# A new order of all engines for a patch-embedding, retention, attention and expert-routing kernel

## The reference

```python
tokens = concat([cls, patches(x) @ W + b]) * pos_embed        # 64 patches of 28x28x3 = 2352 values
h = concat([tokens, txt], axis=1)                             # 97 tokens a sample
a = layernorm(h)
q, k, v = a_heads @ wq, a_heads @ wk, a_heads @ wv            # complex, 8 heads of 16
y = (((q k^T) * decay_mask) v).real                           # causal
yn = groupnorm(y) * gn_scale + gn_bias
h = h + ((silu((a @ w1).real) * yn) @ w2).real
z = layernorm(h); o = softmax(qz kz^T / 4) vz @ Wo + bo       # 8 heads of 16
t = layernorm(z + o) * ln1_g + ln1_b
e = argmax(t @ gate_W + gate_b); gw = max(softmax(...))       # one of 8 experts for each token
h = h + gw * (gelu(t @ W1[e] + b1[e]) @ W2[e] + b2[e])
```

## Time and profile before

| | us |
|---|---|
| three runs | 1279.16, 1279.10, 1278.93 (median 1279.1) |
| profiled execution, own time | 1276.99 |
| its span (first to last instruction) | 1275.0 |
| PE busy | 1240.5 (97%) |
| DVE busy | 998.1 (78%) |
| ACT busy | 794.3 (62%) |
| POOL busy | 410.5 (32%) |
| mean granted TensorE clock | 0.991 |

### The profile page before, as it was taken

How to read it: one execution, slowest core, us unless ns; L and a number is a source line. 1 busy time by engine, 2 the same in 40 slices (tenths; PEclk the granted TensorE clock), 3 DMA queues, 4 the chain that set the end, 5 groups by cost and what they waited for, 6 DMA issues and landing times.

```text
span 1275.0 us, 43269 instructions
## 1 busy us (share of the span) xinstructions
PE 1240.5 (97%) x15924; PEld 930.4 (73%) x15925; DVE 998.1 (78%) x2447; ACT 794.3 (62%) x1787; POOL 410.5 (32%) x268
## 2 busy tenths in 40 slices
PE   8999999999999999999999999999999876999998
PEld 6667777777777777777777777777776556999998
DVE  3678888888888888888888888888888766777776
ACT  2466666666666666666666666666666664556555
POOL 0000322232222222222222222222222146666666
PEclk9999999999999999999999999999999898999999
DMA  9522333333333333333333333333330013443332
GB/s 387 188 83 80 93 93 93 93 93 93 93 93 93 93 93 93 93 93 93 94 92 93 93 93 94 93 93 94 93 93 16 14 17 89 135 114 102 103 103 62
DMA packets 95146, 124.80 MB, mean 98 GB/s; under 512 B 56619, under 2 KB 77149, under 8 KB 94592
## 3 DMA queue, kind: packets, MB, share of 16 engines
q1 hardware_dynamic: 38400, 102.47, 25.4%
q0 software_dynamic: 56576, 19.93, 7.5%
HBM read 101.27 MB, written 20.82 MB: 96 GB/s over the span
## 4 chain that ended last, share of the span: by engine, by line
PE 80%; DVE 6%; issue 5%; DVEq 3%; POOL 2%; DMA 2%; ACT 1%; SPq 0%; POOLq 0%; ACTq 0%
PE bank_emb L479 22%; PE bank_s L550 10%; PE bank_x L564 7%; PE bank_y L460 7%; PE bank_s L637 4%; PE bank_s L614 4%; PE bank_z L460 4%; PE bank_y L649 3%; PE bank_y L667 3%; DVEq L1842 2%; PE bank_z L597 2%; DVE home_x L1846 2%; PE bank_s L460 2%; PE bank_y L690 1%; PE bank_s L843 1%
## 5 line engine op out<-in xcount | busy, mean ns | idle before, releaser
L1909 POOL DMA_INDIRECT expert_rows<-row_sb,placei x128 | 278.1, 2173 | 562.8 <-issue 464.8
L479 PE MATMUL bank_emb<-home_x 128*128 128x256 f32 x1216 | 338.1, 392 | 0.0
L479 PEld LDWEIGHTS bank_emb<-home_x 128*128 128x128 f32 x1216 | 210.3, 189 | 81.9 <-issue 56.5
L1374 DVE TENSOR_TENSOR home_s<-bank_s,con 97x776 f32<-97x776 f32 x256 | 239.3, 956 | 22.9 <-PE bank_s L550 22.8
L1926 POOL DMA_INDIRECT out_tokens<-yo,tok x104 | 122.9, 1181 | 69.7 <-issue 52.7
L1391 DVE TENSOR_REDUCE mx<-bank_s 97x8 f32<-97x776 f32 x128 | 117.7, 961 | 30.8 <-PE bank_s L614 30.6
L1102 ACT ACTIVATE home_s<-bank_s 97x776 f32<-97x776 f32 x128 | 97.5, 814 | 59.5 <-PE bank_s L637 59.5
L550 PE MATMUL bank_s<-qm,xn 32*97 32x452 f32 x1024 | 131.4, 580 | 1.7 <-DVE vp L1381 1.2
L564 PEld LDWEIGHTS bank_x<-home_s,vp 97*32 97x32 f32 x4096 | 90.0, 110 | 33.2 <-issue 29.4
L564 PE MATMUL bank_x<-home_s,vp 97*32 97x97 f32 x4096 | 111.8, 249 | 1.2 <-DVE vp L1381 1.2
L843 PE MATMUL bank_s<-w2e,home_s 128*128 x832 | 109.8, 275 | 0.0
(11 more groups left out here) (297 smaller groups left out, 2369.9 us busy)
## 6 DMA issues: line engine op xcount, KB each, us to landing
home_x<-in_x_main SPq DMA_DIRECT2D x96, 768.0 KB, 4.5
home_x<-expert_rows SPq DMA_DIRECT2D x104, 129.0 KB
w1e<-in_exp_w SPq DMA_DIRECT2D x1, 2576.0 KB, 13.2
txt<-in_txt_t SPq DMA_DIRECT2D x32, 64.0 KB, 3.6
w2e<-in_exp_w SPq DMA_DIRECT2D x1, 2048.0 KB, 17.6
expert_rows<-row_sb,placei POOLq DMA_INDIRECT x128, 8.7
out_tokens<-yo,tok POOLq DMA_INDIRECT x104
home_x<-in_x_tail SPq DMA_DIRECT2D x32, 48.0 KB, 3.4
```

The costliest lines, as they stand in the source:

```text
L479: mm = pe.matmul(banks["emb"][:, 0:NPG], wtok[:, c, :], x_sb[:, c, :], start=(c == 0), stop=(c == KC - 1))
L1374: ins = dve.tensor_tensor(sm[:, k % 2, 2 * h:2 * h + 2, :], pair(h), decay, ALU.mult)
L1909: pool.indirect_dma_start(out=rows[:, :], out_offset=bass.IndirectOffsetOnAxis(ap=placei[:, k, c:c + 1], axis=0), in_=row_sb[:, k, c, E:E ...
```

## The change

Nothing is computed otherwise; the change is in the order of the lists, in the banks and in the form of the loops.

- The cyclic turn has a new order on PE, ACT, DVE and POOL. The first 14 chunks of the embedding of group i+1 stay in turn i, and its last 5 come in the next turn; the retention steps of a group come up to a turn later (lags now up to 5, `c_rank` last). Banks are given anew.
- In PE's turn `c_rank` stands behind `c_rows` and ahead of `a_scores`, where it stood behind a mixing group and ahead of an embedding chunk.
- The cyclic part ends one turn sooner (`STEADY = NG - 1`), and the rest is written out in a new order, longer than before. Semaphore counts of the router come from a list of their own for the rest (`LAST_ROUTE`).
- Two waits are added on DVE: `logits` waits until ACT has read the logits of the group before, and `place_sum` waits for `place_index` of the group before.
- On POOL the text copy stands ahead of the scatter in a turn. At the end the scatters come in the order 27, 28, 31, 30, 29.
- The expert turns are written out on PE, ACT and DVE. The loops of POOL and SP stay.

```diff
+FIRST, LAST = -1, NG + 5
-STEADY = NG
+STEADY = NG - 1
...
+def counts(order, last):
     seen, n = {}, 0
-    for i in range(FIRST, LAST):
+    for i in range(FIRST, STEADY):
...
+    for *what, g in last:
+        n += 1
+        seen[(g, *what)] = n
...
             for i in range(FIRST, STEADY):        # PE, the new turn
+                at(b_scores, i - 3, 1, first=True)
+                at(a_mix, i - 2, 3)
+                at(b_mix, i - 4, 0)
+                at(b_mix, i - 4, 1)
+                at(b_scores, i - 3, 0)
+                at(ahead, i, 14, 15)
+                at(a_var_ahead, i - 1)
+                at(ahead, i, 15, 18)
+                at(a_yvar, i - 2)
+                at(b_max_t, i - 3, 1)
+                at(b_max_t, i - 3, 0)
+                at(b_hrows, i - 3)
+                at(ahead, i, 18, 19)
+                at(a_q_imag, i - 1)
+                at(a_q_real, i - 1)
+                at(b_wo, i - 4)
+                at(b_shifted, i - 3, 1)
+                at(a_out, i - 2)
+                at(c_rows, i - 4, 1)
+                at(c_rows, i - 4, 0)
+                at(c_rank, i - 5)
+                at(a_scores, i - 1, 1, first=True)
+                at(a_gate, i - 1)
+                at(b_values, i - 3)
+                at(b_center, i - 2)
+                at(ahead, i + 1, 0, 2)
+                at(a_scores, i - 1, 0)
+                at(ahead, i + 1, 2, 3)
+                at(b_var, i - 2)
+                at(ahead, i + 1, 3, 7)
+                at(b_shifted, i - 3, 0)
+                at(ahead, i + 1, 7, 10)
+                at(b_k, i - 2)
+                at(ahead, i + 1, 10, 11)
                 at(a_scores, i - 1, 2)
+                at(a_mix, i - 1, 0)
+                at(a_mix, i - 1, 1)
                 at(b_sums, i - 3, 0)
+                at(ahead, i + 1, 11, 12)
                 at(b_q, i - 2)
                 at(a_scores, i - 1, 3)
+                at(a_mix, i - 1, 2)
+                at(b_sums, i - 3, 1)
+                at(ahead, i + 1, 12, 13)
                 at(a_center_ahead, i)
+                at(ahead, i + 1, 13, 14)
...
+            b_wo(NG - 1)                          # PE, the end of the rest
+            c_rank(NG - 3)
+            c_rows(NG - 1, 1)
+            c_rows(NG - 1, 0)
             c_rank(NG - 2)
             c_rank(NG - 1)
...
-            with pe.Fori(2, TURNS1) as n:
+            for n in range(2, TURNS1):
                 turn(n)
...
             def logits(g):
                 dve.wait_ge(s_scaled, g + 1)
+                if g:
+                    dve.wait_ge(s_lexp, g)
...
             def place_sum(g):
                 routed(g, "place_chosen")
+                if g:
+                    routed(g - 1, "place_index")
...
             for i in range(FIRST, STEADY):        # POOL
+                at(text, i + 1)
                 at(scatter, i - 4)
-                at(text, i + 1)
+            scatter(NG - 5)
             scatter(NG - 4)
+            scatter(NG - 1)
+            scatter(NG - 2)
             scatter(NG - 3)
-            scatter(NG - 2)
-            scatter(NG - 1)
```

More of the change, by code:

```diff
@@ new lines, in _ @@
+            embed(NG - 1, 14, 15)
+            a_var(NG - 2)
+            embed(NG - 1, 15, 16)
+            embed(NG - 1, 16, 17)
+            a_yvar(NG - 3)
+            embed(NG - 1, 17, 18)
+            b_max_t(NG - 4, 0)
+            b_max_t(NG - 4, 1)
+            b_hrows(NG - 4)
+            a_q_real(NG - 2)
+            a_q_imag(NG - 2)
+            b_wo(NG - 5)
+            b_shifted(NG - 4, 1)
+            a_out(NG - 3)
+            embed(NG - 1, 18, 19)
+            c_rows(NG - 5, 0)
@@ new lines, in _ @@
+            c_rank(NG - 6)
+            a_scores(NG - 2, 1, first=True)
+            c_rows(NG - 5, 1)
+            b_center(NG - 3)
+            a_gate(NG - 2)
+            b_values(NG - 4)
+            a_scores(NG - 2, 0)
+            b_var(NG - 3)
+            b_shifted(NG - 4, 0)
+            a_mix(NG - 2, 0)
+            b_q(NG - 3)
+            a_scores(NG - 2, 2)
+            b_k(NG - 3)
+            a_mix(NG - 2, 1)
+            b_mix(NG - 4, 0)
+            a_scores(NG - 2, 3)
+            a_mix(NG - 2, 2)
@@ new lines, in _ @@
+            b_sums(NG - 4, 0)
+            b_sums(NG - 4, 1)
+            b_scores(NG - 3, 1, first=True)
+            a_center(NG - 1)
+            a_mix(NG - 2, 3)
+            b_mix(NG - 4, 1)
+            b_scores(NG - 3, 0)
+            a_var(NG - 1)
+            a_yvar(NG - 2)
+            b_max_t(NG - 3, 0)
+            b_max_t(NG - 3, 1)
+            b_hrows(NG - 3)
+            a_q_real(NG - 1)
+            a_q_imag(NG - 1)
+            b_wo(NG - 4)
+            b_shifted(NG - 3, 1)
+            a_out(NG - 2)
@@ L768, in _ @@
+            c_rows(NG - 4, 1)
+            c_rank(NG - 5)
+            a_scores(NG - 1, 1, first=True)
+            c_rows(NG - 4, 0)
+            b_center(NG - 2)
+            a_gate(NG - 1)
+            b_values(NG - 3)
+            a_scores(NG - 1, 0)
+            b_var(NG - 2)
+            b_shifted(NG - 3, 0)
+            a_mix(NG - 1, 0)
+            b_q(NG - 2)
+            a_scores(NG - 1, 2)
             a_mix(NG - 1, 1)
-            b_q(NG - 2)
-            b_mix(NG - 3, 0)
+            b_k(NG - 2)
@@ L865, in _ @@
             second_list()
-            with pe.Fori(2, TURNS1) as n:
+            for n in range(2, TURNS1):
                 turn(n)
             pe.wait_ge(s_list, 2)
-            with pe.Fori(TURNS1, TURNS - 1) as n:
-                turn(n)
-            turn(TURNS - 1, True)
+            for n in range(TURNS1, TURNS):
+                turn(n, n == TURNS - 1)
         @block.scalar
@@ L1242, in hidden @@
                                    bias=w1b[:, s, FF + f:FF + f + 1]).then_inc(s_gelu, 1)
-            for s in range(SLOTS):
-                hidden(0, s)
-            with act.Fori(1, TURNS) as n:
+            for n in range(TURNS):
                 for s in range(SLOTS):
@@ new lines, in _ @@
+            run_on(NG - 5)
+            place_chosen(NG - 5)
+            token_numbers(NG - 3)
+            place_sum(NG - 5)
+            h1_low(NG - 2)
+            a_value_rows(NG - 1, 1, 1)
+            a_value_rows(NG - 1, 1, 0)
+            a_decayed(NG - 1, 1, 0, last=True)
+            a_decayed(NG - 1, 1, 1, last=True)
+            gate_one(NG - 1)
+            b_low(NG - 2)
+            a_value_rows(NG - 1, 0, 1)
+            a_value_rows(NG - 1, 0, 0)
+            a_decayed(NG - 1, 0, 0, last=True)
@@ L1765, in _ @@
             next(first, None)
-            b_normal(NG - 1)
-            next(first, None)
+            next(first, None)
+            next(first, None)
+            b_query_max(NG - 2, 0, 1, last=True)
+            next(first, None)
+            next(first, None)
+            b_normal(NG - 1)
+            first_list_copy()
+            c_sum(NG - 3)
+            b_max(NG - 1, 1, 0)
+            b_max(NG - 1, 1, 1)
+            b_divide(NG - 2)
+            b_query_max(NG - 1, 1, 0)
+            b_query_max(NG - 1, 1, 1, last=True)
@@ L1878, in _ @@
             second_list_copy()
[L1879 removed]
+            for n in range(2, TURNS1 - 1):
                 turn(n)
             dve.wait_ge(s_list, 2)
[L1882 to L1884 removed]
+            for n in range(TURNS1 - 1, TURNS):
+                turn(n, n == TURNS - 1)
             result(TURNS - 1, SLOTS - 1)
```

524 lines of the change are left out of this document (285 added, 239 removed), and 18 rows, old and new, of the table USES.

## The result

The changed kernel takes 1495.3 us (median of four, 1487.4 to 1506.0), against 1279.0 for the kernel before: a ratio of 1.170, 95% interval 1.163 to 1.178. The forecast was 1282.1 with a range of 1273 to 1290. The kernel is 216 us slower, and nothing in the prediction has that size.

A forecast was written before the change was run, and what follows sets the result against it. PE alone was taken to bound the cyclic turns, chains between engines the run-out. Terms -4.3 (to a_residual(31)), -3.2, +11.05 (scatters), +2.5 (clock), -3.0 (expert turns) gave +3.0: 1282.1 us, range 1273 to 1290.

The forecast's parts named there:

- The step that failed: Cyclic turn: waits followed through the new lists, smallest distance about 0.25 us, no stall found.
- Rival B: Cyclic turn: the new turn stalls, one wait of 0.2 us a turn, +5.3 us, 1287.4; chance 0.13.
- The turn of PE: Cyclic turn: cheaper changes of group shape save 0.17 us a turn, 31.50 for 31.67, -4.4 us over 26 turns.
- Start: Before the first a_residual: ten more embedding chunks, +4.3 us, and a wait for group 2's pixels, +2.0.
- the clock: First expert turns: PE's idle time brings the lower clock for some 6 us, costing 2.5 us (bounds 0 to 3.2).
- Run-out: Residual 29 to 31: 53.3 us for 58.1; from there to the first expert transpose 34.7 for 37.9, -3.2.
- rival A: Run-out gives back much more than counted, 11.5 of 17.2 idle us, time 1274.3; chance 0.20.
- POOL's scatters: Ahead of the first output: twelve scatters behind place_index(31), 30.4 to 30.6 us in place of 19.4, +11.05 us.
- Two readings beside it: Slow PE work after idle time: line 460 matmuls 1.66 us against 0.65, and a lone group at 1060.36.
- Expert turns written out: Expert loops: nine loop boundaries of 0.38 us go, 3.4 us, taken as -3.0 (bounds 0 to -4).
- The page weighed: Scatter train: the skill's port-lock rule would add some 4.8 us, near 1287; the prediction did not use it.
- The sum by the row: Scatter train: each scatter keeps its 2.15 us beside DVE's copies and DVE pays, so 1282 rather than 1287.

The follow-up runs named there:

- experiment 1: Changed kernel with four row buffers in place of three, the small table moved to make room: 1297.5 us, ratio 1.014 to the kernel before.
- experiment 4: Changed kernel with four row buffers and POOL's last scatters in the order 29, 30, 31: 1289.9 us, ratio 1.010 to the kernel before.
- experiment 2: Changed kernel with three row buffers, DVE's router placement done at once behind place_all and run_on: 1304.8 us, ratio 1.020 to the kernel before.
- experiment 6: Changed kernel with four row buffers, last scatters in the order 29, 30, 31 and experts' weights loaded behind group 2: 1290.4 us.
- last run of experiment 8: Changed kernel with four row buffers, weights behind group 2 and the last eight scatters dealt out among outputs: 1283.6 us, ratio 1.006 to the kernel before.
- experiment 8: Kernel before with expert turns written out and the last eight scatters dealt out, one behind every fourth output of turns 1 to 4: 1273.1 us, ratio 0.9965.
- experiment 5: Kernel before with its expert turns written out on PE, ACT and DVE, nothing else changed: 1275.0 us, ratio 0.9984.

## Why the prediction was wrong

**The step that failed** is the one that reads "Followed through the new lists, with the durations of before, the smallest distance is about 0.25 ... and I find no stall". It followed the waits of PE for DVE and ACT and of banks, and left out a wait whose releaser is a DMA: ACT's row copy for a scatter of three groups earlier. In the kernel before it never shows, so no row of before names it, and I took a wait without a row for one that costs nothing. The distances were in the trace all the same: the last scatter at 516.29, the row copy at 551.70, and 10.2 to 12.5 us to land. (Part 6 of its profile page has 8.7, but that is the median over all four scatters of a group, and the wait is for the last.) The change moves the router back against the attention and `place_index` from the head of DVE's list to its middle. From the first scatter of group 12 to the row copy of group 15 there were 42.8 us (508.92 to 551.70). In experiment 1, where nothing waits, there are 13.2 (545.88 to 559.09), and 5.8 from the last scatter, where landing needs some 12. The missing 6 us are what ACT waits each turn, 5.99 in the one shown.

**Rival B** ("the new turn stalls ... one wait of 0.2 a turn") had the place, the new turn, but neither the wait nor the scale. I sized it by the smallest slack, as if a stall could only be as large as an error of my count. A wait that closes a loop isn't a lost slack: it sets the period of the whole turn.

**The turn of PE** was right: 31.47 in experiment 1 for a forecast of 31.50, so the -0.17 is there (-0.20). `c_rank` takes 0.11 in that run's chain (532.18 to 532.29), as assumed; which other changes of shape gave the rest was not tested. It didn't come through: between groups 3 and 29 only -1.3 of -5.2 is left. Five turns of experiment 1 are longer by 0.4 to 1.0 us, one of experiment 4 by 2.1. That one is a wait of PE for nothing that the profile shows:

```profile
270.18 0.94 PE L647 MATMUL bank_s<-k,q 32*97 32x194 f32 x16 [2.03 <-issue]
```

The kernel before has none in 26 turns. The same matmuls wait 0.93 us in experiment 1, 0.58 in experiment 2 and 1.21 in experiment 6, and not at all in the last run of experiment 8: it belongs to this place of the program, but not with one size. What it is stays open; that the instructions arrive late there is a candidate that no run tests.

**Start.** The forecast of +6.3 became +9.6. The first `a_residual` has 21 more embedding matmuls ahead of it (114 against 93), the ten chunks and a bit that the sum has. The DMA wait is as forecast (1.88 us at 38.91, for +2.0). Two more of 1.24 and 1.25 us, for ACT's queries at 35.16 and 60.67, were not in it; but the kernel before has 2.3 us of other waits in its start (0.46, 0.94, 0.63 and 0.28), so all waits together grew by 2.3, about what the sum has. The rest is the clock: in this trace it is at the lower level for 3.4 us behind the wait for the pixels. In experiments 2 and 4, where it isn't, the start is +7.7 and +7.9. The last 1.5 us are not taken apart.

**Run-out.** In the changed kernel two more waits for a row buffer, 7.0 and 5.6 us of PE, stand in it. With four buffers it gives back 2.1 of the forecast 4.8, and the stretch to the first transpose costs 2.1 where 3.2 were to be gained: 96.0 us from residual 29 to the first transpose, for 88.0 forecast and 96.0 before. This is half of the 15 us that experiment 1 leaves, and it isn't the chance of one trace: the order of before takes 95.2 to 96.3 us there in four traces, the new one 96.0 to 97.1 in four of five with four buffers, at a granted clock of 0.87 to 0.89, and 91.6 in the fifth (experiment 4), at 0.97. PE has ten chunks less to do there, and stands idle longer instead: 19.3 us with four buffers, 17.2 before. `b_scores`, `b_shifted` and the last `c_rank` (4.06 idle us, 4.51 in the earlier trace rows) wait for ACT and DVE as before. The hand count erred to the good side here, so rival A was the wrong way round.

**POOL's scatters** were right in mechanism and size. Twelve DMAs behind `place_index(31)`, the first output 32.8 us after the first of them (forecast about 30.5), since one break of 3.0 us lies in it, ahead of 1287.71:

```profile
1269.69 2.51 POOL L2096 DMA_INDIRECT expert_rows<-row_sb,placei  x1 [33.67 <-issue]
...
1282.32 2.40 POOL L2096 DMA_INDIRECT expert_rows<-row_sb,placei  x1 [0.31 <-issue]
1287.71 2.15 POOL L2096 DMA_INDIRECT expert_rows<-row_sb,placei  x1 [3.00 <-issue]
...
1300.00 2.15 POOL L2096 DMA_INDIRECT expert_rows<-row_sb,placei  x1 [0.30 <-issue]
1302.45 1.00 POOL L2114 DMA_INDIRECT out_tokens<-yo,tok  x1 [0.30 <-issue]
```

DVE waits 15.6 us for the landing of slot 0's output (2.23 in the earlier trace rows), and PE 15.1 us, and then eight matmuls of line 931 take 2.08 us instead of 1.06:

```profile
1310.89 0.15 DVE L2045 COPY tok<-home_x 128x1 int32<-128x1 int32 x1 [15.63 <-DMA out_tokens<-yo,tok]
...
1380.41 0.35 DVE L2047 SCALAR_TENSOR_TENSOR yo<-home_s,home_x 128x128 f32<-128x128 f32 x1
...
1382.31 0.35 DVE L2047 SCALAR_TENSOR_TENSOR yo<-home_s,home_x 128x128 f32<-128x128 f32 x1
```

```profile
1312.42 2.08 PE L931 MATMUL bank_x<-home_s,home_x 128*128 128x128 f32 x8 [15.13 <-DVE home_x L2034]
```

The stretch is +14.8 in the changed kernel and +11.7 with four buffers, against 11.05. Turn 1 then takes 16.7 us against 14.7 in experiment 5, so the clock costs 2.0 (2.5 in the sum). Two readings beside it were wrong, though neither is a term of the sum: the lone `c_rank` at 1060.36 in the earlier trace rows isn't slow, it takes 0.18 us in the middle of the kernel too (at 500.55 in experiment 1); and 1.66 us from a timeline was set against 0.65 from the chain, where the timeline has 0.81.

**Expert turns written out.** The two `yo` rows show the tile at 1.90 us; the longer step of the earlier trace rows is gone. From the ninth result to the end the changed kernel takes 1.3 us less than before, which with the clock's 2.0 is 3.3 for the loops, as in the trace of experiment 5 (3.0 in the sum). The size is right by luck in part: only 1.8 of it come from turns 3 to 11, and 0.7 from turn 1, which had no loop on PE and DVE before (experiment 5).

**The page weighed.** The sum by the row was right: in the changed kernel ten of the twelve scatters take 2.14 to 2.16 us with DVE's copies beside them, and the copies pay, with up to 1.24 us instead of 0.48. But the other direction exists too. The two longer ones, 2.51 and 2.40 us, start 0.08 and 0.11 us after a weight copy of DVE has started, and so, within 0.05 us, do the four of 2.47 to 2.50 among the eight scatters dealt out in experiment 8. Not every scatter with a copy under way is longer, so the rows don't give a rule; what it costs here is 0.25 to 0.36 us a scatter. The Trainium skill, "SBUF — State Buffer", section "SBUF: two separate sides", says that such a copy of DVE locks GpSimd out of the port pair that they share, so that it can't write descriptors. The trace agrees in that direction only by these few tenths, 0.6 us for the twelve scatters, where the sum by the page had 4.8.

## What to carry to other kernels

When a software pipeline is reordered, list every wait of every engine with its releaser and the number of turns between them, the waits that cost nothing now above all, and for those released by a DMA add issue and landing time; then sum each closed loop through a buffer ring and compare it with the turn. Work that is moved out of an engine's way still takes its time where it goes: the scatters moved whole cost 4.4 us from the first transpose to the end, and dealt out they cost what they had cost before, no more and no less. So read the stretch in which the edit acts in both traces before a median is called a gain. And a saving of 0.2 us a turn should be tested alone, before it is bought with a longer start and a new run-out.

## What was not expected of the hardware

The scatters of one group (four indirect DMAs) take 10.8 to 13.3 us from the issue of the last to the release of the waiting copy in the cyclic part of the changed kernel, more than the 8.4 and 8.85 us of an output tile behind such trains. DVE's weight copy, 0.48 us alone, took up to 1.81 us beside an indirect DMA of POOL. And PE stood 2.0 us at 270.18 without any releaser in the profile, at a place where kernels with the new turn wait and the kernel before doesn't.
